# An audio block with a mixture of experts on one core: the expert loop goes from two rounds deep to three

## The reference, cut to what matters

```python
logits = xf @ Wr + br                       # (8064, 64)
topk_logits, topk_idx = jax.lax.top_k(logits, 2)
gates = jax.nn.softmax(topk_logits, axis=1)
combine = zeros((T, E)).at[arange(T)[:, None], topk_idx].add(gates)
for e in range(64):
    h = relu(xf @ W1[e] + b1[e])            # 64 -> 128
    y = h @ W2[e] + b2[e]                   # 128 -> 64
    out = out + combine[:, e:e + 1] * y
```

## Time and profile before

| | |
|---|---|
| median of three executions | 828.19 us (827.23 to 837.27) |
| the profiled execution's own time | 836.15 us |
| its span in the trace | 834.3 us |
| mean granted TensorE clock, share of full speed | 0.802 |
| TensorE matmul busy | 485.4 us (58%) |
| TensorE weight load busy | 314.4 us (38%) |
| VectorE busy | 559.4 us (67%) |
| ScalarE busy | 318.9 us (38%) |
| GpSimd busy | 597.6 us (72%) |
| mean DMA rate | 102 GB/s |

### The profile page before, as it was taken

How to read it: one execution, slowest core, us unless ns; L and a number is a source line. 1 busy time by engine, 2 the same in 40 slices (tenths; PEclk the granted TensorE clock), 3 DMA queues, 4 the chain that set the end, 5 groups by cost and what they waited for, 6 DMA issues and landing times.

```text
span 834.3 us, 8865 instructions
## 1 busy us (share of the span) xinstructions
PE 485.4 (58%) x2514; PEld 314.4 (38%) x2520; DVE 559.4 (67%) x1180; ACT 318.9 (38%) x582; POOL 597.6 (72%) x393
## 2 busy tenths in 40 slices
PE   4735144575557665755764855888777893784000
PEld 3734011222222222222443433766665672673000
DVE  1597799999999999999754735444554561336311
ACT  2159856556646655452340411223322331231000
POOL 5995769999999999995066636566665636663774
PEclk9968569879898779787856666899999996997555
DMA  7999970000000000000045002688988894852211
GB/s 237 382 197 126 85 5 0 0 1 0 0 0 0 0 0 0 0 0 1 1 117 144 22 14 86 176 242 235 255 241 242 244 285 116 234 163 85 74 38 27
DMA packets 106604, 84.95 MB, mean 102 GB/s; under 512 B 30464, under 2 KB 90240, under 8 KB 106560
## 3 DMA queue, kind: packets, MB, share of 16 engines
q1 hardware_dynamic: 79312, 54.76, 30.3%
q10 hardware_dynamic: 19184, 21.40, 8.6%
q0 software_dynamic: 8064, 8.27, 4.0%
HBM read 57.22 MB, written 33.49 MB: 109 GB/s over the span
## 4 chain that ended last, share of the span: by engine, by line
PE 27%; DVE 20%; POOL 19%; issue 16%; ACT 8%; another core or an unknown queue 5%; SPq 1%; ACTq 1%; DMA 0%; POOLq 0%; DVEq 0%
PE ps L903 8%; POOL x_w L578 7%; POOL w_ring L571 6%; PE ps L894 6%; POOL xt L651 5%; DVE hh_ring L1408 4%; PE ps L885 3%; PE ps L676 2%; ACT ps L1057 2%; DVE w_ring L1402 2%; ACT ps L1063 2%; PE ps L740 2%; DVE w_ring L1387 2%; DVE x_w L1584 1%
## 5 line engine op out<-in xcount | busy, mean ns | idle before, releaser
L740 PE MATMUL ps<-x_w,ident 128*128 128x512 f32 x252 | 151.8, 760 | 102.4 <-POOL x_w L578 102.4
L630 POOL DMA_INDIRECT sorted_rows<-xp,slot_i x126 | 122.0, 968 | 106.3 <-issue 32.5
L651 POOL DMA_INDIRECT xt<-expert_out,slot_i x126 | 122.4, 972 | 78.3 <-issue 32.3
L571 POOL TENSOR_TENSOR w_ring<-xt,bc 128x2016 f32<-128x2016 f32 x32 | 143.1, 4472 | 13.5 <-DVE hh_ring L1408 7.3
L1408 DVE TENSOR_TENSOR_SCAN hh_ring<-ps,w_ring 128x1024 f32<-128x1024 f32 x64 | 145.8, 2278 | 0.1
L578 POOL TENSOR_TENSOR x_w<-hh_ring,bc 128x2016 f32<-128x2016 f32 (+1 forms) x32 | 140.7, 4397 | 1.0 <-PE ps L740 1.0
L740 PEld LDWEIGHTS ps<-x_w,ident 128*128 128x128 f32 x252 | 59.2, 245 | 197.7 <-POOL x_w L578 125.7
L1063 ACT ACTIVATE ps<-dt_t,a_exp 128x1024 f32<-128x1024 f32 x64 | 71.5, 1117 | 64.2 <-DVE hh_ring L1408 64.2
L1057 ACT ACTIVATE ps<-dt_t,a_exp 128x1024 f32<-128x1024 f32 x64 | 71.6, 1118 | 52.1 <-DVE w_ring L1387 52.1
L1152 ACT ACTIVATE x_w<-ps 128x512 f32<-128x512 f32 x40 | 23.9, 597 | 145.0 <-remote 50.3
L1387 DVE TENSOR_TENSOR w_ring<-ps,w_ring 128x1008 f32<-128x1008 f32 x64 | 76.7, 1199 | 3.4 <-ACT ps L1057 3.4
(11 more groups left out here) (209 smaller groups left out, 890.1 us busy)
## 6 DMA issues: line engine op xcount, KB each, us to landing
dt_t<-packed SPq DMA_DIRECT2D x140, 96.5 KB
x_w<-packed SPq DMA_DIRECT2D x112, 96.5 KB
x_w<-sorted_rows ACTq DMA_DIRECT2D x40, 256.0 KB
expert_out<-x_w ACTq DMA_DIRECT2D x80, 128.0 KB
sorted_rows<-pad_rows SPq DMA_DIRECT2D x2, 3584.0 KB, 24.2
bc<-packed SPq DMA_DIRECT2D x68, 96.5 KB
packed<-in_L_ffn_W SPq DMA_DIRECT2D x3, 2048.0 KB, 41.9
x_w<-in_x SPq DMA_DIRECT2D x7, 448.0 KB, 9.5
```

The source lines that it names most:

```text
L571: pool.tensor_tensor(w_buf(k, 2), up3[:, bass.ds(c * DC, DC), 1:S].unsqueeze(1).broadcast_to([P, 2, DC, L]), vec_of(k, 2), ALU.mult).then_ ...
L630: pool.indirect_dma_start(out=sorted_rows[h], out_offset=bass.IndirectOffsetOnAxis(ap=slot_i[:, c, l:l + 1], axis=0), in_=xn[:, l, :], in_ ...
L651: pool.indirect_dma_start(out=y[:, l, :], out_offset=None, in_=expert_out[h], in_offset=bass.IndirectOffsetOnAxis(ap=slot_i[:, c, l:l + 1] ...
L740: ins = pe.matmul(ps[:, i, :], ident[:, :], src[:, i * BANK:(i + 1) * BANK], start=(k < 0), stop=(k == (N - 2 if last else N - 1)), skip_g ...
```

## The change

The loop is three rounds deep. `DEPTH = 3`, `LAG_H` goes from 2 to 3 and `LATE` from 4 to 6. A round k uses the two banks k % 3 and 3 + k % 3: the first holds what ScalarE reads (that round's turned rows in columns 0 to 255, and the hidden values of one tile of each pair), the second what VectorE reads (the other hidden values, and the outputs). Gates and biases get banks 6 and 7. TensorE waits before round k for round k - 3 of ScalarE and VectorE. `rows_T` turns two pairs in every round and `xT_copy` copies 256 columns in every round. The output matmuls are 64 columns wide. The bias chain starts at rounds 16 and 20 in place of 13 and 15. The weight ring has 25 places, and `hT_e` moves to `w_ring`. As `LATE` stands in `keep_pace`, GpSimd's waits are for a count that is higher by 2. The diff, without the comments and blank parts:

```diff
--- before.py
+++ after.py
@@ -60,16 +60,17 @@
 NPROJ = C + 2 * N
 H_CR, HCP_CR, ADD_CR, G_CR, H2_CR = 4, 4, 2, 1, 1
 RING = 4
-XRING = 8
+XRING = 10
 WRING = XRING + 15
 YRING = 4
-LAG_H, LATE = 2, 4
-TURNED, ADDED = 13, 15
+DEPTH = 3
+LAG_H, LATE = DEPTH, 2 * DEPTH
+TURNED, ADDED = 16, 20
 STEPS = [-(-n // 2) for n in PAIRS]
 PAIR0, UNIT0, STEP0 = ([sum(v[:h]) for h in range(len(SHARES) + 1)] for v in (PAIRS, UNITS, STEPS))
 WROW = HID + C + 1
 BLOCK = 4 * P * WROW
-OUT = 2 * C
+OUT = C
 CQ = -(-L // 8)
 IDS = 32
@@ -240,11 +241,11 @@
         hc_ring = x_w1[:, o:o + 4 * U].rearrange("p (k n) -> p k n", k=4)
         rows_in = x_w1[:, o:o + RING * UNIT * P].rearrange("p (k q n) -> p k q n", k=RING, n=P)
         o += RING * UNIT * P
-        xT_e = x_w1[:, o:o + 2 * UNIT * P].rearrange("p (k q n) -> p k q n", k=2, n=P)
-        o += 2 * UNIT * P
-        hT_e = x_w1[:, o:o + 8 * P].rearrange("p (k t q n) -> p k t q n", k=2, t=2, n=P)
-        o += 8 * P
+        xT_e = x_w1[:, o:o + 2 * DEPTH * P].rearrange("p (k q n) -> p k q n", k=DEPTH, n=P)
+        o += 2 * DEPTH * P
         y_e = x_w1[:, o:o + YRING * 4 * C].rearrange("p (k q t d) -> p k q t d", k=YRING, q=2, d=C)
+        o = 3 * BANK
+        hT_e = w_flat[:, o:o + 4 * DEPTH * P].rearrange("p (k t q n) -> p k t q n", k=DEPTH, t=2, n=P)
         y1 = xt[:, 0:L * C].rearrange("p (l d) -> p l d", d=C)
         y2 = xt[:, L * C:2 * L * C].rearrange("p (l d) -> p l d", d=C)
@@ -360,6 +361,18 @@
         def vec_of(k, n=1):
             return bc[:, k:k + n, 1:S].unsqueeze(2).broadcast_to([P, n, DC, L])
+        def bank_of(k):
+            return ps[:, k % DEPTH, :], ps[:, DEPTH + k % DEPTH, :]
+
+        def rows_home(i, j, n=1):
+            return bank_of(i)[0][:, j * P:(j + n) * P]
+
+        def hidden_home(i, t, j):
+            return bank_of(i + LAG_H)[t][:, (2 * (1 - t) + j) * P:(2 * (1 - t) + j + 1) * P]
+
+        def outputs_home(i, a, z):
+            return bank_of(i + LATE)[1][:, 2 * P + a * OUT:2 * P + z * OUT]
+
         def w_of(n):
             return w_places[n % WRING]
@@ -878,11 +891,14 @@
             pe.wait_ge(s_tei, len(SHARES))
-            def rows_T(u):
-
-                pe.wait_ge(s_rows[u % RING], 16 * (u // RING + 1))
-                for q in range(UNIT):
-                    last = pe.transpose(ps[:, 0, q * P:(q + 1) * P], rows_in[:, u % RING, q, :], ident[:, :])
+            def rows_T(i):
+
+                for j, n in enumerate(pairs_of(i)):
+                    u = unit_of(n)
+                    if in_share(n) % UNIT == 0:
+                        pe.wait_ge(s_rows[u % RING], 16 * (u // RING + 1))
+                    last = pe.transpose(rows_home(i, j), rows_in[:, u % RING, in_share(n) % UNIT, :],
+                                        ident[:, :])
                 return last
             def hidden(i):
@@ -891,44 +907,44 @@
                     pe.wait_ge(s_win[n % WRING], 32 * (n // WRING + 1))
                 for j, n in enumerate(pairs_of(i)):
                     for t in range(2):
-                        last = pe.matmul(ps[:, 2 + 2 * (i % 2) + t, j * P:(j + 1) * P],
+                        last = pe.matmul(hidden_home(i, t, j),
                                          w_of(n)[t * C:(t + 1) * C, t, 0:HID],
-                                         xT_e[t * C:(t + 1) * C, i // 2 % 2, 2 * (i % 2) + j, :], start=True, stop=True)
+                                         xT_e[t * C:(t + 1) * C, i % DEPTH, j, :], start=True, stop=True)
                 return last
             def outputs(i):
                 for j, n in enumerate(pairs_of(i)):
                     for t in range(2):
-                        last = pe.matmul(ps[:, 6 + i % 2, (2 * j + t) * OUT:(2 * j + t + 1) * OUT], hT_e[:, i % 2, t, j, :],
+                        last = pe.matmul(outputs_home(i, 2 * j + t, 2 * j + t + 1), hT_e[:, i % DEPTH, t, j, :],
                                          w_of(n)[:, t, HID + C - OUT:HID + C], start=True, stop=True)
                 return last
             def gates_T(q):
                 for j in range(4):
-                    last = pe.transpose(ps[:, 1, j * P:(j + 1) * P],
+                    last = pe.transpose(ps[:, 6, j * P:(j + 1) * P],
                                         comb[0][:, 8 * q + 2 * j:8 * q + 2 * j + 2, :].rearrange("p l e -> p (l e)"), ident[:, :])
                 return last
             def bias_of(q):
                 for j in range(4):
-                    last = pe.matmul(ps[:, 1, j * P:(j + 1) * P], cT[:, q % 2, j * P:(j + 1) * P], b2w[:, :],
+                    last = pe.matmul(ps[:, 7, j * P:(j + 1) * P], cT[:, q % 2, j * P:(j + 1) * P], b2w[:, :],
                                      start=True, stop=True)
                 return last
             pe.wait_ge(s_b2, 32)
-            rows_T(0).then_inc(s_pstep, 2)
-            for k in range(2, STEP0[-1] + LATE):
-                pe.wait_ge(s_astep, k - LAG_H + 1)
+            for k in range(STEP0[-1] + LATE):
+                if k >= LAG_H:
+                    pe.wait_ge(s_astep, k - LAG_H + 1)
                 if k >= LATE:
                     pe.wait_ge(s_dstep, k - 2 * LAG_H + 1)
                     last = outputs(k - LATE)
-                if k < STEP0[-1] + LAG_H:
+                if LAG_H <= k < STEP0[-1] + LAG_H:
                     last = hidden(k - LAG_H)
-                if k % 2 == 0 and k < STEP0[-1]:
-                    last = rows_T(k // 2)
+                if k < STEP0[-1]:
+                    last = rows_T(k)
                 if group_at(k, TURNED) is not None:
                     last = gates_T(group_at(k, TURNED))
                 if group_at(k, ADDED) is not None:
@@ -1147,18 +1163,15 @@
             act.activation(top[:, 1, :], top[:, 0, :], ACT.Exp).then_inc(s_eexp, 1)
-            def xT_copy(u):
-
-                return act.activation(xT_e[:, u % 2, :, :].rearrange("p q n -> p (q n)"), ps[:, 0, :], ACT.Copy)
-
-            def cT_copy(q):
-
-                return act.activation(cT[:, q % 2, :], ps[:, 1, :], ACT.Copy)
+            def xT_copy(i):
+
+                m = len(pairs_of(i))
+                return act.activation(xT_e[:, i % DEPTH, 0:m, :].rearrange("p q n -> p (q n)"), rows_home(i, 0, m), ACT.Copy)
             def relu_A(i):
                 for j, n in enumerate(pairs_of(i)):
-                    last = act.activation(hT_e[:, i % 2, 0, j, :], ps[:, 2 + 2 * (i % 2), j * P:(j + 1) * P], ACT.Relu,
+                    last = act.activation(hT_e[:, i % DEPTH, 0, j, :], hidden_home(i, 0, j), ACT.Relu,
                                           bias=w_of(n)[:, 0, HID + C:WROW])
                 return last
@@ -1177,25 +1190,27 @@
                     act.wait_ge(s_disp[h], 16 * 2 * (SHARES[h][1] - SHARES[h][0]))
                 load_rows(act, u)
-            def next_rows(u):
-
-                if u + RING < UNIT0[-1]:
-                    rows_of_unit(u + RING)
+            def next_rows(i):
+
+                d = i + 1
+                u = d // (UNIT // 2) - 1 + RING
+                if d % (UNIT // 2) == 0 and u < UNIT0[-1]:
+                    rows_of_unit(u)
             for v in range(RING):
                 rows_of_unit(v)
-            act.wait_ge(s_pstep, 2)
-            xT_copy(0).then_inc(s_astep, 2)
-            next_rows(0)
-            for k in range(2, STEP0[-1] + LAG_H):
+            for k in range(STEP0[-1] + LAG_H):
                 act.wait_ge(s_pstep, k + 1)
-                if k % 2 == 0 and k < STEP0[-1]:
-                    xT_copy(k // 2)
+                if k < STEP0[-1]:
+                    last = xT_copy(k)
+                if k >= LAG_H:
+                    last = relu_A(k - LAG_H)
                 if group_at(k, TURNED) is not None:
-                    cT_copy(group_at(k, TURNED))
-                relu_A(k - LAG_H).then_inc(s_astep, 1)
-                if k % 2 == 0 and k < STEP0[-1]:
-                    next_rows(k // 2)
+                    q = group_at(k, TURNED)
+                    last = act.activation(cT[:, q % 2, :], ps[:, 6, :], ACT.Copy)
+                last.then_inc(s_astep, 1)
+                if k < STEP0[-1]:
+                    next_rows(k)
                 if k > LATE:
                     store(k - LATE - 1)
             for i in range(STEP0[-1] + LAG_H - LATE - 1, STEP0[-1]):
@@ -1581,7 +1596,7 @@
             def relu_B(i):
                 for j, n in enumerate(pairs_of(i)):
-                    last = dve.tensor_scalar(hT_e[:, i % 2, 1, j, :], ps[:, 3 + 2 * (i % 2), j * P:(j + 1) * P],
+                    last = dve.tensor_scalar(hT_e[:, i % DEPTH, 1, j, :], hidden_home(i, 1, j),
                                              w_of(n)[:, 1, HID + C:WROW], 0.0, ALU.add, ALU.max)
                 return last
@@ -1591,7 +1606,7 @@
                 if i >= YRING:
                     dve.wait_ge(s_st[i % YRING], 16 * (i // YRING))
                 return dve.tensor_copy(y_e[:, i % YRING, 0:m].rearrange("p q t d -> p (q t) d"),
```

(4 more changed lines are left out.)

## The result

The changed kernel takes 840.27 us (median of 20 executions) against 832.04 for the kernel before (20), a ratio of 1.0083 with a 95% interval of 1.0058 to 1.0107. The forecast was 819 us with a range of 800 to 834, so it was wrong in direction and in range: the change costs 0.8% where a gain of 1% was expected. About 4 us of the miss are the base, as the forecast started from 828.19 us, the median of three executions. All medians here are of all executions, and all ratios are of the fast ones alone, which leaves out those more than 1.5% above the fastest of their kernel (five of the changed kernel's twenty), so that a ratio can differ from the quotient of the medians beside it.

What follows compares the result with a forecast made beforehand. GpSimd's DMA queue with its pauses was taken as the bound. Depth -10, start +2, store wait -0.5 and end -0.5 sum to -9 us, giving 819 us on the median of 828.19, range 800 to 834.

Steps and rivals of the forecast that it cites:

- What bounds the kernel: Expert loop: GpSimd's DMA queue sets the time, with 34 pauses, as its DMAs hold back TensorE's increments.
- Outputs 64 columns wide: TensorE's output matmuls: -0.2 us a round, hidden under GpSimd's DMAs, so worth 0 in the cycle.
- the cover: Loop cycle: TensorE's three rounds fit into GpSimd's 8.65 us for six DMAs, by 1.0 to 1.6 us.
- the point of decision: Loop: TensorE at its lower clock sets the cycle once three rounds take over 7.5 us.
- Depth, -10 us through 25 pauses: Loop's `keep_pace` waits: three rounds shown per release, mostly six DMAs a run, 25 pauses for 34, -10 us.
- rival 1: Loop: no third round passes a held increment, 34 pauses stay; 827 to 832 us, chance 0.18.
- Start +2: Loop start: two more rounds before GpSimd's first paced DMA, between -2 and +4, taken as +2 us.
- end and store wait -1: Second share's store wait -0.5 us; after the last release, one more of five rounds holds only outputs, -0.5 us.
- Weights, rows, copies, banks at 0: Loop's weight ring, row loads, `xT_copy` copies and bank layout: each claimed to cost nothing, 0 us.
- Rival 3: Loop: longer idle pieces drop TensorE to its lower clock, 4.0 us a round; 840 to 890 us, chance 0.09.
- sign of 0.8: Profile after: a TensorE clock below 0.8 in the loop would show it had fallen to its lower clock.

Runs made afterwards that it cites:

- e14: Kernel before with all gathers moved after the loop's last round, increments held while GpSimd issues DMAs: 887.20 us (one execution) against 831.59.
- e13: Changed kernel with output matmuls 128 columns wide again, three rounds deep, increments held: 824.94 us against 831.59 for the kernel before, ratio 0.9943.
- e2: Changed kernel with output matmuls 128 columns wide again, three rounds deep, increments not held: 753.82 us against 754.09 for the kernel before, ratio 1.0008.
- e12: Kernel before with only the output matmuls narrowed to 64 columns, two rounds deep, for a second trace: 771.09 us against 752.27, ratio 1.0265.
- e1: Kernel before with only the output matmuls narrowed to 64 columns, two rounds deep: 771.17 us against 754.09, ratio 1.0154.
- e9: Kernel before, unchanged, run for its trace, increments not held: 752.88 us (one execution).
- e5: Changed kernel itself, rerun where increments aren't held: 767.04 us against 753.16 for the kernel before, ratio 1.0184.
- e7: Changed kernel plus one 256-column matmul a round whose result is overwritten: 760.20 us against 752.85 for the kernel before, ratio 1.0089.

## Why the prediction was wrong, point by point

- **What bounds the kernel** was right: GpSimd's queue with its pauses, and increments held while its own DMAs go (e14). It was right for the held condition; free, the kernel before has no pauses at all and takes 753 us.
- **"Outputs 64 columns wide ... worth 0 in the cycle; it widens the cover"** is the step that failed. It was sized at -0.2 us of TensorE's time a round; measured -0.06 (1.00 for 1.06); the eight weight loads, of 128 columns each, take 0.97 us in both kernels. And it did not widen the cover but took it away: the clock in the paced stretch went from 0.94 to 0.73, a round at the lower level takes 3.37 us, and three of them 10.1, more than the 7.5 named as the point of decision. The term was +15 us (840.27 against e13's 824.94) where it stood at 0.
- **Depth, -10 us through 25 pauses**: the pauses lost 4.1 us (33.9 for 38.0 in e13's trace), and by another way; there are 33 of them. The whole change but for the width is worth -4.7 us by e13's ratio (0.0057 x 832) and -6.7 by its medians, where the sum had -9. A third round does not get past held increments whole; rival 1 had this right, with the earlier trace rows as its evidence, and I argued it away with one cycle in which TensorE was not stopped. That cycle shows one round, 20 records, past the increment of 643.79, and then TensorE's own wait at a depth of two; in e13 it stops 22 records after 590.74, so the cycle could not tell. Rival 1's time of 827 to 832 was still too high, as it gave nothing for TensorE's going on at the release. Free, depth is worth nothing (four intervals about 1).
- **Start +2, end and store wait -1**: in the changed kernel's trace +1.5 at the first paced DMA, -0.5 for the last wait, -2.3 for the store wait. With pauses +6.1 this gives +4.8; the span grew by 4.1. These terms were right within 2 us.
- **Weights, rows, copies, banks at 0**: nothing speaks against it; e2 has all of them and equals the kernel before.
- **Rival 3**, with a chance of 0.09, is what came: the clock in the loop is under its sign of 0.8, and 840.27 lies at the edge of its 840 to 890. It had half of the cause. Idle pieces of TensorE do come before each fall, in both kernels (six falls each in the paced part and just behind it). But longer idle pieces through depth are not what made the difference: the wide variant, with the same depth, keeps 0.92 in the paced stretch when held. What it left out is that with narrow outputs the clock stays low while TensorE is not idle at all (40.5 us in e12). By what the width sets how long a fall lasts, about 3 us in e2 and 40.5 in e12, no run shows. Rival 3's price was 4.0 us a round and +85 us if the clock stayed low throughout. Its upper value for the outputs, 2.1 us, stands in the earlier trace rows (2.08 us; the clock is 0.50 from 700 to 705 us of that trace); at 0.50 the narrow ones took 1.81, and measured were 3.37 us a round at the lower level, for about half of the paced stretch.

## What to carry to other kernels

Spare columns in a matmul need not be waste: before narrowing one, look at the granted clock of the stretch and not only at the matmul's time, since here 64 columns fewer saved 0.06 us a round and, where the clock stayed low with them, cost up to 1.4 (3.37 us a round at the lower level against the 1.93 of the kernel before at full clock). When the clock falls, ask two things of the trace: what the engine did just before (here it was idle, for 1.4 to 2.4 us in e1, e2 and e12), and how long the clock takes to come back (about 3 us in e2, 40.5 in e12). Here the deeper pipeline paid only where the engine that sets the pace had pauses (0.6% with GpSimd's 34, nothing without them); if that engine is a DMA queue, count its pauses before and after. And test each part of a change alone: here one part gains 0.6% where increments are held, and the other turned it into a loss.

## What the runs showed of the hardware

- The same kernel takes 753 or 832 us on the same chip, in different comparisons. In the traces of the comparisons with 832 (its own, e13, e14) TensorE's semaphore increments are held while GpSimd issues indirect DMAs, and in that of the kernel at 753 (e9) they aren't: 2.6 us from the transposes' end to ScalarE's start against 0.03. Held, they arrive 2.0 to 2.25 us after the start of a run's last DMA (2.00 in e13, 2.11 and 2.25 in the earlier trace rows); ScalarE's and VectorE's weren't seen to be (TensorE goes on 0.23 us after VectorE's copy, at 641.40). The cause is open.
- After the first held increment TensorE itself goes on for one round and a piece of the next, and then stops between two matmuls that have no wait between them (in e13 22 matmul records after 590.74 us, with the stop before 593.72).
- TensorE's clock falls after idle pieces of 1.4 to 2.4 us (e1, e2, e12) with outputs of either width. With 128 columns it was back after 3.0 to 3.5 us in 23 of 27 falls; with 64 it stayed at the lower of its two levels for 40.5 us (e12) and 75 us (e1) in which TensorE was never idle.
- At the loop's start, with TensorE never idle from 497 to 532 us, the clock is at 0.50 with 64-column outputs (e5) and at 1.00 with the same loop and 256 more columns a round (e7).
